# Second feed-forward of three chunks placed among the score groups of attention, with 32x32 turns on VectorE

## The reference, cut to what matters

```
ffn(x):  y1 = ln1(x + mha(x))          # each row attends to itself only: a linear map
         gates = softmax(y1 @ wg)      # 8 experts, the best one is taken
         place = running count of rows per expert; keep if place < 256
         y  = keep * gate * expert(y1) # two linear layers without nonlinearity
         return ln2(y1 + y)
attn(x): 16 heads of 8, keys from a latent of 64, rotary; pages of 32 rows:
         a row sees its own page and all before it
x = x + 0.5 * ffn(norm(x))
x = x + attn(norm(x))
x = x + 0.5 * ffn(norm(x))
```

## Time and profile before

| | |
|---|---|
| median of three runs | 495.75 us |
| the profiled execution's own time | 495.45 us |
| its span, first to last instruction | 493.7 us |
| mean granted TensorE clock | 0.925 |
| busy: PE, DVE, ACT, POOL | 391.1, 167.9, 356.5, 110.4 us |
| first exponential of attention starts | 161.88 us |

### The profile page before, as it was taken

How to read it: one execution, slowest core, us unless ns; L and a number is a source line. 1 busy time by engine, 2 the same in 40 slices (tenths; PEclk the granted TensorE clock), 3 DMA queues, 4 the chain that set the end, 5 groups by cost and what they waited for, 6 DMA issues and landing times.

```text
span 493.7 us, 7548 instructions
## 1 busy us (share of the span) xinstructions
PE 391.1 (79%) x2749; PEld 150.2 (30%) x2749; DVE 167.9 (34%) x631; ACT 356.5 (72%) x551; POOL 110.4 (22%) x203
## 2 busy tenths in 40 slices
PE   2799999236661898888888888888888887789990
PEld 1798544122220222222121121111121111655540
DVE  2524487639666031111010010101010000668885
ACT  1324567435231899999999999999999998356761
POOL 2532578830000000000000000000000000477785
PEclk9869999759775799999999999999999999999996
DMA  6930920001888980000000000000000000000001
GB/s 134 385 147 15 115 33 1 0 1 64 180 217 212 230 132 3 2 1 1 1 1 1 0 2 1 1 0 1 2 0 1 1 0 2 1 0 3 21 23 42
DMA packets 23172, 24.44 MB, mean 50 GB/s; under 512 B 2364, under 2 KB 20348, under 8 KB 22876
## 3 DMA queue, kind: packets, MB, share of 16 engines
q1 hardware_dynamic: 23132, 23.92, 20.7%
HBM read 16.51 MB, written 7.41 MB: 48 GB/s over the span
## 4 chain that ended last, share of the span: by engine, by line
ACT 26%; PE 19%; issue 18%; DVE 9%; POOL 3%; DVEq 0%; ACTq 0%; POOLq 0%
ACT arena L543 24%; PE ps L1025 7%; PE ps L1009 3%; PE ps L1034 2%; PE ps L947 2%; PE ps L922 1%; DVE arena L716 1%; PE ps L926 1%; DVE longest L700 1%; DVE stats L553 1%; DVE arena L729 1%; ACT arena L507 1%; DVE arena L734 1%; POOL arena L444 1%; PE ps L857 1%
## 5 line engine op out<-in xcount | busy, mean ns | idle before, releaser
L543 ACT ACTIVATE arena<-ps 128x1024 f32<-128x1024 f32 x272 | 251.3, 1129 | 13.4 <-PE ps L1009 13.3
L1025 PE MATMUL ps<-arena,v_st 128*9 128x512 f32 (+3 forms) x1280 | 144.8, 534 | 29.0 <-ACT arena L543 28.9
L1009 PE MATMUL ps<-packed 51*128 51x512 bf16 (+4 forms) x640 | 85.2, 353 | 5.6 <-issue 5.3
L435 POOL TENSOR_TENSOR arena<-x_tm,lnb 128x512 f32<-128x512 f32 x8 | 10.0, 1267 | 317.2 <-DVE x_tm L571 317.1
L776 DVE COPY o_sb<-ps 128x512 f32<-128x512 f32 x16 | 11.1, 692 | 187.4 <-PE ps L1025 187.4
L1009 PEld LDWEIGHTS ps<-packed 51*128 51x128 bf16 (+1 forms) x640 | 20.4, 95 | 106.0 <-ACT arena L543 94.9
L1025 PEld LDWEIGHTS ps<-arena,v_st 128*9 128x9 f32 x1280 | 20.6, 89 | 97.3 <-ACT arena L543 86.9
L507 ACT ACTIVATE arena<-ps,arena 128x128 f32<-128x128 f32 x128 | 36.1, 367 | 11.5 <-PE ps L922 10.3
L646 DVE SCALAR_TENSOR_TENSOR arena<-ps,arena 128x128 f32<-128x128 f32 x128 | 35.3, 343 | 13.2 <-ACT arena L507 7.7
L926 PE MATMUL ps<-w,arena 128*128 128x512 f32 x64 | 33.1, 599 | 0.4 <-DVE arena L646 0.3
L922 PE MATMUL ps<-w,arena 128*128 128x512 f32 x64 | 33.2, 601 | 0.1
(11 more groups left out here) (119 smaller groups left out, 397.8 us busy)
## 6 DMA issues: line engine op xcount, KB each, us to landing
packed<-piece_dram SPq DMA_DIRECT2D x16, 384.0 KB
piece_dram<-arena SPq DMA_DIRECT2D x8, 384.0 KB, 6.8
packed<-in_w1T SPq DMA_DIRECT2D x8, 256.0 KB, 4.7
packed<-in_w SPq DMA_DIRECT2D x8, 256.0 KB, 4.9
trio<-in_rope SPq DMA_DIRECT2D x2, 1024.0 KB, 7.9
piece_dram<-arena SPq DMA_DIRECT2D x8, 256.0 KB, 6.8
packed<-in_template SPq DMA_DIRECT2D x4, 480.0 KB, 12.5
x_tm<-in_x SPq DMA_DIRECT2D x4, 256.0 KB, 5.0
```

What stands on the lines that cost most here:

```text
L543: nc.scalar.activation(pexp[:, n % PB, :], ps[:, at:at + 2, :].rearrange("p b n -> p (b n)"), ACT.Exp, scale=SCALE).then_inc(exp_done, 1)
L1009: ins = pe.matmul(ps[:, 2 * (n % SLOTS) + b, col:col + w], packed[rows, 1, pair, P * j:P * (j + 1)], packed[rows, 0, pair, q:q + w], start ...
L1025: ins = pe.matmul(ps[32 * h:32 * h + VW, 6 + k % OB, q - GW * c:q - GW * c + w], v_st[:, j, GH * g + h, :], pexp[:, n % PB, 512 * b + col: ...
```

## The change

The second feed-forward of chunks 0, 1 and 2 is issued inside attention. After certain groups of the blocks of chunks 1, 2 and 3 (`SLOT_AT`) TensorE does one step of it: for each early chunk O, P, L, R, K, B and then, for each of its four tiles, H (high half of the experts) and E (low half), 42 steps in 44 slots. The step uses the output bank that the running block does not use (`EARLY_BANK`); TensorE first waits until the step before it in the same block has been read (`early_read`), or for the block output to have been taken. The first values matmuls of a block wait for the last early step of the block before.

ScalarE keeps only the gate exponential of these chunks, behind the fifth exponential after the group of L (`EXP_AFTER`). What it did otherwise goes to VectorE (coefficient copy, bias copy, scaling of the high experts) and to GpSimd (both normalisations, and the scale and final addition of the second norm). The steps A and C of these chunks, turns on TensorE, become `turn_rows` on VectorE: sixteen turns of 32 partitions by four tiles by 32 columns each. The block output is turned in 32x32 blocks straight out of PSUM and divided; at the end of a chunk a second such turn gives `oT`. `turn_output`, `attn_tm` and U are gone. The rows of wo are loaded in another order to suit, in four DMAs. Before their early parts, VectorE and GpSimd wait until all pieces of queries and keys have been stored, since the new buffers lie over them. After attention `feed_forward(1)` does chunk 3 alone; VectorE first does the output statistics of chunk 2. Buffers of the second feed-forward (`y1T`, `prod`, `pair`, `quad`, `coef` and others) get a second place outside the exponentials' buffers. The helper functions of the steps are the old code, moved, with the bank as an argument.

```diff
+EARLY = G - 1
+SLOT_AT = {1: (1, 4), 2: (1, 3, 5, 9), 3: (1, 4, 7, 9, 12)}
+SLOT_GROUPS = [min(m for m in range(len(GROUPS)) if GROUPS[m][0] == k) + at
+               for k in range(NG, len(BLOCKS)) for at in SLOT_AT[BLOCKS[k][0]]]
+EARLY_STEPS = [(step, i) for g in range(EARLY)
+               for step, i in [(s, g) for s in "OPLRKB"] + [(s, t) for t in range(GT * g, GT * (g + 1)) for s in "HE"]]
+assert len(SLOT_GROUPS) >= len(EARLY_STEPS)
+EARLY_AT = list(zip(SLOT_GROUPS, EARLY_STEPS))
+EARLY_BANK = {step: 7 - GROUPS[m][0] % OB for m, step in EARLY_AT}
+EXP_AFTER = {LAST_UNIT[m] + SLOTS + 2: i for m, (step, i) in EARLY_AT if step == "L"}
+
...
-        "pe": "U0 U1 O0 U2 A0 U3 P0 O1 O2 A1 O3 P1 C0 L0 A2 E0 R0 E1 K0 C1 B0 L1 P2 A3 E2 E3 R1 P3 K1 E4 B1 C2 "
-              "E5 L2 E6 E7 R2 C3 K2 E8 L3 B2 E9 R3 E10 E11 K3 E12 B3 E13 E14 E15",
-        "act": "U0 U1 U2 A0 U3 A1 M0 C0 L0 A2 M1 E0 K0 C1 E1 B0 L1 A3 E2 E3 M2 K1 E4 B1 C2 E5 M3 L2 E6 E7 V0 K2 "
-               "C3 E8 L3 B2 E9 E10 V1 E11 K3 E12 B3 E13 E14 E15 V2",
-        "dve": "O0 X0 P0 O1 X1 O2 O3 P1 L0 X2 R0 X3 K0 E0 L1 E1 P2 R1 E2 K1 E3 P3 E4 Z0 L2 E5 R2 E6 K2 E7 F0 L3 "
-               "E8 R3 Z1 E9 K3 E10 F1 E11 E12 Z2 E13 E14 E15 F2 Z3 F3",
-        "pool": "B0 X0 P0 X1 B1 B2 P1 X2 X3 B3 E0 E1 P2 E2 E3 P3 E4 Z0 E5 E6 E7 E8 Z1 E9 E10 E11 E12 Z2 E13 E14 "
-                "E15 Z3",
+        "pe": "O3 A3 P3 C3 L3 R3 K3 B3 E12 E13 E14 E15",
+        "act": "A3 M3 C3 L3 K3 B3 E12 E13 E14 E15",
+        "dve": "O3 X3 P3 L3 R3 K3 E12 E13 E14 E15 Z3 F3",
+        "pool": "X3 P3 B3 E12 E13 E14 E15 Z3",
...
-            for dst, src in ((wqo[:, 0, :], a["wq"]), (wqo[:, 1, :], a["wo"]), (wdu[:, 0, :], a["w_downT"]),
+            for dst, src in ((wqo[:, 0, :], a["wq"]), (wdu[:, 0, :], a["w_downT"]),
                              (wdu[:, 1, :], a["wk_up"]), (wdu[:, 2, :], a["wv_up"])):
                 sp.dma_start(dst, src).then_inc(att_in, 16)
+            for h in range(GH):
+                sp.dma_start(wqo[VC * h:VC * (h + 1), 1, :],
+                             a["wo"].rearrange("(g h d) n -> h g d n", g=NG, h=GH)[h]).then_inc(wo_in, 16)
...
+            def normalise(kind, n, g):
+
+                pool.wait_ge(ln_offset[kind], 2 * (normed_groups(kind) * n + g) + 2)
+                for t in range(GT * g, GT * (g + 1)):
+                    ins = pool.tensor_scalar(y[:, t, :], y[:, t, :], rstd[:, t:t + 1], offset[:, t:t + 1], ALU.mult, ALU.add)
+                ins.then_inc(normed[kind], 1)
...
+            pool.wait_ge(piece_out, 16 * 2 * STORE_DMAS * G)
+            for g in range(EARLY):
+                ln_rsqrt(ROWS, 1, g)
+                add_bias(1, g)
+                ln_rsqrt(LN1, 1, g)
+                normalise(LN1, 1, g)
+                for t in range(GT * g, GT * (g + 1)):
+                    add_experts(1, t)
+                ln_rsqrt(LN2, 1, g)
+                normalise(LN2, 1, g)
+                pool.wait_ge(normed[LN2], EARLY + g + 1)
+                pool.tensor_tensor(y[:, group(g), :], y[:, group(g), :], rows_of(lnb[:, 0, :]), ALU.mult).then_inc(z_part, 1)
+                pool.wait_ge(z_part, G + g + 1)
+                pool.wait_ge(xb_ready, G + g + 1)
+                pool.tensor_tensor(x_tm[:, group(g), :], y[:, group(g), :], xb[1][:, group(g), :], ALU.add).then_inc(x_new[2], 1)
             feed_forward(1)
...
+                if n in EXP_AFTER:
+                    gate_exp(1, EXP_AFTER[n])
...
-            for k, (c, g) in enumerate(BLOCKS):
-                b = k % OB
+            def take_output(k):
+
+                c, g = BLOCKS[k]
                 dve.wait_ge(pv_done, LAST_GROUP[k] + 1)
-                dve.tensor_copy(o_sb[:, b, :], ps[:, 6 + b, :]).then_inc(o_copied, 1)
+                if k:
+                    dve.wait_ge(o_read, k)
+                dve.transpose(o_t[:].rearrange("p t v -> p (t v)"), ps[:, 6 + k % OB, :]).then_inc(o_turned, 1)
                 dve.wait_ge(o_turned, k + 1)
-                turned_o = ps[:, 6 + b, :].rearrange("p (t h v) -> p t h v", h=GH, v=VC)
-                dve.reciprocal(den[:, b, :, :], turned_o[:, :, :, HD]).then_inc(den_ready, 1)
+                dve.reciprocal(den[:], o_t[:, :, HD]).then_inc(den_ready, 1)
                 dve.wait_ge(den_ready, k + 1)
-                dst = attn_tm[:, group(c), GH * HD * g:GH * HD * (g + 1)]
-                dve.tensor_tensor(dst.rearrange("p t (h d) -> p t h d", d=HD), turned_o[:, :, :, 0:HD],
-                                  den[:, b, :, :].unsqueeze(3).to_broadcast([P, GT, GH, HD]),
-                                  ALU.mult).then_inc(o_read, 1)
+                if g == 0 and c:
+                    dve.wait_ge(copied[OUT], c)
+                dve.tensor_tensor(attn_n[:, :, HD * g:HD * (g + 1)], o_t[:, :, 0:HD],
+                                  den[:].unsqueeze(2).to_broadcast([P, GW // VC, HD]), ALU.mult).then_inc(o_read, 1)
+                if g == NG - 1:
+                    dve.wait_ge(o_read, k + 1)
+                    dve.transpose(oT[:, cols(c)], attn_n[:].rearrange("p t v -> p (t v)")).then_inc(copied[OUT], 1)
+
+            def turn_rows(kind, g, src, dst):
+
+                for down in range(P // VC):
+                    for across in range(P // VC):
+                        to = dst[VC * across:VC * (across + 1), cols(g)].rearrange("p (t b r) -> p t b r", b=P // VC, r=VC)
+                        ins = dve.transpose(to[:, :, down, :], src[VC * down:VC * (down + 1), group(g), VC * across:VC * (across + 1)])
+                ins.then_inc(copied[kind] if kind == ROWS else turned[kind], 1)
+
+            def early(step, i):
+
+                bank, q, k = EARLY_BANK[step, i], G + i, T + i
+                if step == "O":
+                    add_attention(i, bank)
+                    row_stats(1, i)
+                    turn_rows(ROWS, i, x_tm, xT)
+                elif step == "P":
+                    add_mha(1, i, bank)
+                elif step == "L":
+                    sub_max(1, i, bank)
+                elif step == "R":
+                    keep_expert(1, i, bank)
+                elif step == "K":
+                    dve.wait_ge(coef_mm, q + 1)
+                    dve.tensor_copy(coefT[:, i, :], ps[0:TE, bank, P * (2 + i % 2):P * (3 + i % 2)]).then_inc(coefT_ready, 1)
+                elif step == "B":
+                    dve.wait_ge(bias_mm, q + 1)
+                    dve.tensor_copy(base_rows(1, i), bank_tiles(bank)).then_inc(bias_read, 1)
+                elif step == "H":
+                    dve.wait_ge(high_mm, k + 1)
+                    if i >= 2:
+                        dve.wait_ge(pair_ready, k - 1)
+                    for e in range(E // 2, E):
+                        cut = slice(D * (e - E // 2), D * (e - E // 2 + 1))
+                        ins = dve.tensor_scalar(prod[1][:, i % 2, cut], ps[:, bank, cut], coef[1][:, i, e:e + 1], None, ALU.mult)
+                    ins.then_inc(high_ready, 1)
+                elif step == "E":
+                    low_experts(1, i, bank)
+
+            dve.wait_ge(piece_out, 16 * 2 * STORE_DMAS * G)
+            for m in range(len(GROUPS)):
+                if m in LAST_GROUP:
+                    take_output(LAST_GROUP.index(m))
+                for at, (step, i) in EARLY_AT:
+                    if at == m:
+                        if step == "R":
+                            pick_expert(1, i)
+                        if step == "O" and i:
+                            out_stats(1, i - 1)
+                        if step == "L":
+                            dve.wait_ge(normed[LN1], G + i + 1)
+                            turn_rows(Y1, i, y, y1T[1])
+                            dve.wait_ge(turned[Y1], G + i + 1)
+                            dve.tensor_scalar(y1T[1][:, cols(i)], y1T[1][:, cols(i)], g1c[:, 0:1], g1c[:, 1:2],
+                                              ALU.mult, ALU.add).then_inc(copied[Y1], 1)
+                        early(step, i)
+            out_stats(1, EARLY - 1)
...
-                    pe.wait_ge(o_read, k - OB + 1)
+                    pe.wait_ge(o_turned, k - OB + 1)
+                if first and k - 1 in LAST_EARLY:
+                    early_read(*LAST_EARLY[k - 1])
...
-            def turn_output(k):
-
-                pe.wait_ge(o_copied, k + 1)
-                for j in range(GT):
-                    ins = pe.transpose(ps[:, 6 + k % OB, P * j:P * (j + 1)], o_sb[:, k % OB, P * j:P * (j + 1)], ident[:])
-                ins.then_inc(o_turned, 1)
+            LAST_EARLY = {GROUPS[m][0]: step for m, step in EARLY_AT}
+
+            def early_read(step, i):
+
+                done, count = {
+                    "O": (x_new[1], i + 1), "P": (mha_read, G + i + 1),
+                    "L": (logit_sub, G + i + 1), "R": (kept, G + i + 1),
+                    "K": (coefT_ready, G + i + 1), "B": (bias_read, G + i + 1), "H": (high_ready, T + i + 1),
+                    "E": (pair_ready, T + i + 1)}[step]
```

(73 more changed lines are left out.)

311 lines of the change are left out of this document (153 added, 158 removed).

## The result

The changed kernel takes 531.45 us as the median of four runs, the kernel before 495.01 us in the same session. In the ratio, disturbed executions of both are left out: 1.0664, 95% interval 1.058 to 1.0749. The profiled execution took 526.82 us with a span of 524.9 us, against 495.45 and 493.7. The forecast was slower, at 509 us with a range to 523: the sign was right, the rise between the profiled executions was 31 us instead of 13, and the range missed.

A forecast was written before the change was run, and what follows sets the result against it. Attention was taken to be paced by ScalarE's exponentials, with TensorE following with little room. From 495.45 us, attention would grow by 41.3 and the tail shrink by 28.0, giving 509 us, range 487 to 523.

The forecast's parts named there:

- old turns removed: Attention: fifteen of the sixteen old four-transpose steps on TensorE go, at 0.21 us each, -3.2 us.
- H and E, 24: Attention: 24 early expert steps hold TensorE for 0.86 us and cost ScalarE 0.49 each, 11.8 us.
- own matmuls of O, P, L, B; gate: Attention, three early chunks: O, P and L add 4.7 us, B steps 4.7, gate exponentials on ScalarE 0.7.
- waits at P, L, R: Attention: TensorE waits for data from VectorE and GpSimd, mainly 4.2, 6.2 and 5.0 us at L; 16.6 us in all.
- clock after L: Attention: TensorE returns from each long wait at the low clock, 2 us three times, 6.0 us, ends 0 and 9.
- L chain: VectorE and GpSimd work between P's matmul and L's data: 10.2 us, said to be 7.5 with every low end.
- B: Rival, chance 0.15: the work between P and L fits between slots, so TensorE never waits; 486 us.
- 17u: Slot distance in attention: 17 times u, the 0.92 us per ScalarE exponential; with added steps, 18.1 us to chunk 1's L.
- The room: Attention: TensorE's slack for one added step before ScalarE is delayed, 0.58 - 0.21 = 0.37 us.
- C: Rival, chance 0.13: the waits stand but TensorE's clock never falls, in attention or tail; 498 us.
- D: Rival, chance 0.10: VectorE and GpSimd slow each other, pieces 0.28 us and normalisations 0.8; 518 us.
- 4.9 us of low clock in the tail: Tail: chunk 3 alone leaves TensorE idle, so steps C, L, R, K, B run at half clock, adding 4.9 us.

The follow-up runs named there:

- e_dve: Kernel before with only the block-output turn moved to VectorE and wo loaded in the other order, no early feed-forward; ratio 0.9856 to the kernel before.
- e_warm: Changed kernel with five extra 512-column matmuls on TensorE before each early logits step waits for its data; ratio 1.0576 to the kernel before.
- e_half: Changed kernel with eight of the sixteen turned pieces of y left out in each early chunk; 517.62 us profiled against 526.82.
- e_sched: Changed kernel with the same 42 early steps in the same order, put after other groups; median 496.24 us, ratio 1.0019 to the kernel before.
- e_narrow: Changed kernel with 256 instead of 512 columns in each of the 24 early expert matmuls; ratio 1.0411 to the kernel before.
- e_double: Changed kernel with each of the 24 early expert matmuls issued twice; median 547.41 us, ratio 1.107 to the kernel before.
- e_sched_tail: e_sched with chunk 2's output norm moved behind chunk 3's first norm on VectorE and GpSimd; ratio 0.994 to the kernel before.
- e_busy_tail: e_sched_tail with two and six extra 512-column matmuls in TensorE's waits in the tail; ratio 0.9897 to the kernel before.

## Why the prediction was wrong in size

**The mechanism and the sign were right.** The steps run inside attention; the longest gaps stand before the logits and VectorE ends them; the clock is low behind them; the tail was forecast at 48.5 us and took 47.9; its first expert scaling came 31.6 us into it (508.60), in the range that I gave. That the tail fits to 0.6 us is in part luck: its expert matmuls began 29.6 us in (506.65) instead of 32.4, and from there to the end took 18.3 us instead of 16.1.

**Terms of attention**, forecast and measured. Measured prices count the lost overlap, 0.10 us for each interruption:

| | forecast | measured | from |
|---|---|---|---|
| old turns removed | -3.2 | -4.8 | e_dve |
| H and E, 24 | 11.8 | 19.0 | 0.79 each |
| own matmuls of O, P, L, B; gate | 10.1 | 13.7 | 9 times 0.82, 3 times 1.87, 0.7 |
| waits at P, L, R | 16.6 | 24.6 | the rest of their gaps |
| clock after L | 6.0 | 6.3 | three times the 2.1 of L0 in e_warm, an estimate |
| start of attention | 0 | 1.5 | below |
| sum | 41.3 | 60 | 60.2 measured |

The waits are what is left of the gaps at these steps, so the closing sum does not test this term; e_half and e_sched test the waits.

**Failed term: the waits ("I take 0.20, nearest to the smaller tile: 3.2").** A piece takes 0.31 us in a row of sixteen, 5.04 us where my upper end was 4.5. I had taken the price from columns, and between rows of 64 and 128 columns leaned to the smaller, although each piece has 128. The excess of 1.8 us falls on each L, where TensorE waited 5.91, 7.75 and 6.84 us against 4.2, 6.2 and 5.0. It falls on the turns of the early rows as well: it makes the 1.88 us at P0, where 0.3 was forecast, and the 1.62 at P2, where nothing was. Of the 8.0 us by which this term was short, 4.6 lie at the L steps and 3.4 at P0 and P2. e_half measures it alone: 2.5 us less turning in each chunk, 7.0 us less attention. e_sched, which takes away waits and clock together, made attention 32.3 us shorter; the two terms of the table make 30.9.

GpSimd's share was near its forecast: 1.76 us for four normalisations, a mean of 0.453 for a 128x128 operation with one tensor input, against 0.46 for the two-input add of the earlier trace rows. The Trainium skill (GPSIMD Engine Reference, Engine selection) has one-input operations near line rate and two-input ones about twice as slow as VectorE's. At 128x128 the trace shows no difference between the two kinds; at 128x512 a two-input operation takes 1.27 us on GpSimd (L505) against 0.69 on VectorE (L624, one input in PSUM), which agrees with the second part.

Smaller slips stand in this term. The low ends of the L chain add to 7.75 us, not 7.5, which does not help B. And the distances to L1 and L2, 18.1 and 20.0 us, are 1 us more than 17u and 19u with the three steps at the prices of the forecast; with the measured prices the first comes out (277.53 to 295.72 in the trace, 18.2). VectorE's addition at P1 was not held by GpSimd either, though nearly: TensorE released it at 291.44, the rstd had been ready at 290.97.

**Failed term: the price of a step ("costs ScalarE e - 0.37").** Two mis-sizings of the same kind add up. The room is about 0.27, not 0.37: I read the idle time (0.21) as the cost of the old step, while its cost includes the lost overlap, 0.10 more; e_dve gives 0.32 for it. And the hold of a lone float32 matmul of 512 columns is 1.06, not 0.86: I took the pace of matmuls that follow each other. In the tail of the kernel before, the weights for the matmul of 478.71 begin to load at 478.28; those of the lone one load at 337.20, with its start. That this makes the 0.20 us is a reading, which no run tested. 1.06 - 0.27 = 0.79 per step fits the H step above; the slopes between e_narrow, after and e_double are 0.42 and 0.88 us for each 0.43 and 0.86 us of columns.

**Smaller terms.** Waiting for all piece stores was not quite free: VectorE took the first block output at 174.39, released by a store, and the values of block 2 waited 1.78 us for it, 1.1 us of it seen by ScalarE. The forecast gave that cover at most 1 us; with the lost overlaps it cost 1.5. The wait for the rstd of chunk 3 in the tail was forecast at 4 us; e_sched_tail takes 2.6 off the tail of e_sched (49.7 to 47.2).

**The rivals.** B needed a chain of 6 us after P; it was 12.1 (196.37 to 208.44). C is refuted by the logits at 1.84 and the values at 1.90. D named the right item, turned pieces at 0.28, for a wrong reason: sixteen take 5.04 us at 202.66, when GpSimd has nothing to do, and 5.02 at 377.15, beside its two-input operations, so the pieces are that long by themselves. Its 518 would still have been too low, as it kept the room of 0.37. On the turn itself, the rows have 0.58 us on TensorE against 5.04 on VectorE for a 128x512 turn; with the rule of the Trainium skill (VectorE: DVE Perf Modes, Rules for kernel authors), to turn 128x128 on TensorE, the trace agrees. Early turns on TensorE were not run: by e_dve four transposes would cost ScalarE about 0.32 us, an estimate, and need a copy out of PSUM.

**Where the gain went.** With the waits scheduled away, an early chunk costs attention (282.3 - 250.5) / 3 = 10.6 us and saves the tail (74.5 - 47.2) / 3 = 9.1 us. In the schedules measured here, moving the feed-forward into attention is no gain (with the extra matmuls of e_busy_tail, 10.7 against 9.5), and e_sched leaves no long wait to be scheduled away: TensorE's free time per group is 0.27 us and an expert step needs 1.06. What remains of the gain is the block-output turn. Fewer than three early chunks were not tried.

**Open.** Whether all 4.9 us of low clock in the tail can be had: e_busy_tail got 1.1 and lost the clock again before the bias matmuls. And why a turned piece has 0.31 us; no run changed its shape.

## What to carry to other kernels

Before moving work into another stage's gaps, compare the piece with the free time of the engine that carries it, per period, not over the stage: what TensorE had idle was 0.27 us at a time. Count a slot's distance in time against the whole chain that feeds it, and keep slots apart by the chain's length rather than evenly. Read the cost of an interruption from the start times of what is interrupted, not from its idle time.

## What the runs showed of the hardware

- Exponentials of 128x1024 follow each other every 0.917 us (268 in 246.01) though one alone takes 1.02: each break in the row costs its idle time and 0.10 us.
- VectorE's 32x32-block turn: 0.71 us for 128 partitions by 512 columns, from PSUM (L860) or SBUF (L870), but 0.31 us for 32 partitions by 128 columns. Sixteen small ones cost seven times a wide one for the same data.
- A lone 512-column float32 matmul between values and score matmuls holds TensorE for 1.06 us, two in a row for 1.92.
- Five matmuls put into a wait of TensorE (e_warm) had three outcomes. With 1.30 us of idle time left behind them (L0) the logits, scores and values that followed ran at the full level; with 2.23 (L2) only the first of them did; with 3.15 (L1) none did, and the fill was worth 0.1 us.
